# Weights of five more expert batches loaded before the expert stage, into the space of the residual and of the routing's row buffers

## The reference

```
E, K, I, CAP = 64, 8, 96, 64
probs = softmax(x @ gate_w.T);  w, sel = top_k(probs, K);  w = w / sum(w)
pos  = place of (token, expert) in its expert's queue;  valid = pos < CAP
xin[e, slot] = x[tok]                                   # 64 rows of each expert
h    = silu(xin @ wg) * (xin @ wu)                      # 256 -> 96
out  = h @ wd                                           # 96 -> 256
y[tok] += out[e, slot] * w * valid
return x + y
```

## Time and profile before

| | before |
|---|---|
| median of 3 runs | 1032.08 us (1030.96 to 1032.15) |
| profiled execution | 1035.25 us |
| its span in the trace | 1033.4 us |
| busy share of the span | PE 84%, DVE 65%, PEld 65%, ACT 41%, POOL 32% |
| DMA, SP's queue (plain) | 46.62 MB, 15.7% of 16 engines' span |
| DMA, POOL's queue (gathers and scatters) | 9.44 MB, 5.1% |

### The profile page before, as it was taken

The page is one execution under the profiler, slowest core; times in us unless marked ns, Lnnn a source line. Parts: engine busy times, 40 slices in busy tenths (PEclk is TensorE's granted clock), DMA queues, the critical chain, the costliest instruction groups (busy, mean ns, idle before and its releaser), DMA issues. The chain is left out here.

```text
span 1033.4 us, 25740 instructions
## 1 busy us (share of the span) xinstructions
PE 870.1 (84%) x9240; PEld 673.2 (65%) x9240; DVE 676.8 (65%) x1581; ACT 424.2 (41%) x1011; POOL 335.0 (32%) x293
## 2 busy tenths in 40 slices
PE   0799999999999899999889999999998840396881
PEld 0577777777777688998667777777776730264650
DVE  5577777777877665555367777777775589364560
ACT  1243444444434333324355566655556740021220
POOL 1443443434433040000133333333332010354763
PEclk9899999999999999999999999999999875598996
DMA  9300000000000000000011111111110396287542
GB/s 296 88 12 17 15 10 15 15 10 15 12 13 31 2 11 1 0 0 0 3 17 27 30 30 30 30 30 28 26 29 29 102 342 182 64 238 198 82 78 30
DMA packets 74906, 56.61 MB, mean 55 GB/s; under 512 B 40944, under 2 KB 70000, under 8 KB 74864
## 3 DMA queue, kind: packets, MB, share of 16 engines
q1 hardware_dynamic: 68720, 46.62, 15.7%
q0 software_dynamic: 6144, 9.44, 5.1%
HBM read 41.81 MB, written 14.22 MB: 54 GB/s over the span
## 5 line engine op out<-in xcount | busy, mean ns | idle before, releaser
L402 ACT ACTIVATE pr_t<-bank 128x512 f32<-128x512 f32 x128 | 76.4, 597 | 160.7 <-PE bank L298 159.9
L822 POOL TENSOR_TENSOR g_k_bd<-g_k_t,head_mask 128x1024 f32<-128x1024 f32 x32 | 60.6, 1895 | 134.8 <-ACT g_k_t L997 134.8
L310 PEld LDWEIGHTS bank<-v_bd,pr_t 128*64 128x64 f32 x2048 | 70.0, 137 | 26.5 <-issue 26.3
L298 PE MATMUL bank<-ident,sub 128*128 128x128 f32 x512 | 82.5, 284 | 3.6 <-ACT pr_t L402 2.9
L310 PE MATMUL bank<-v_bd,pr_t 128*64 128x18 f32 x2048 | 82.8, 214 | 0.1
L298 PEld LDWEIGHTS bank<-ident,sub 128*128 128x128 f32 x512 | 56.1, 141 | 31.3 <-issue 17.6
L479 DVE TENSOR_TENSOR sub<-bank,top 128x2048 f32<-128x2048 f32 x32 | 73.3, 2292 | 3.9 <-DVE top L475 0.2
L259 POOL TENSOR_TENSOR rot<-part_a,part_b 128x512 f32<-128x512 f32 x32 | 40.8, 1274 | 103.7 <-DVE part_b L488 103.7
L475 DVE TENSOR_REDUCE top<-bank 128x32 f32<-128x2048 f32 x32 | 73.1, 2285 | 0.6 <-PE bank L286 0.4
L817 POOL TENSOR_TENSOR xres<-xres,g_out_bias 128x256 f32 (+1 forms) x32 | 23.4, 731 | 152.4 <-DVE g_xn L1020 152.4
L646 ACT ACTIVATE f_hid<-bank,b 128x128 f32<-128x128 f32 x128 | 36.6, 368 | 85.4 <-PE bank L592 85.4
(11 more groups left out here) (196 smaller groups left out, 2040.0 us busy)
## 6 DMA issues: line engine op xcount, KB each, us to landing
e_w_gu<-in_experts_in SPq DMA_DIRECT2D x16, 768.0 KB, 9.0
e_w_d<-in_experts_out SPq DMA_DIRECT2D x16, 384.0 KB, 10.5
table<-r_row SPq DMA_DIRECT2D x16, 320.0 KB, 9.1
xres<-in_x SPq DMA_DIRECT2D x4, 1024.0 KB, 9.8
out<-xres SPq DMA_DIRECT2D x32, 128.0 KB, 1.7
keys_in<-in_ctx_t SPq DMA_DIRECT2D x32, 64.0 KB, 1.8
vals_in<-in_ctx_t SPq DMA_DIRECT2D x32, 64.0 KB, 1.8
w<-in_L_ffn_w SPq DMA_DIRECT2D x2, 1024.0 KB, 8.1
```

The source lines that it names most:

```text
L298: m = pe.transpose(b_pr[:, j * P:(j + 1) * P], sub[:, v, cols], k.ident[:, :])
L310: m = pe.matmul(b_o[64 * b:64 * b + 64, hp * VW0:(hp + 1) * VW0], pr_t[:, e, j, b * S:(b + 1) * S], v_bd[:, v, b, hp, :], start=True, stop ...
L402: act.activation(pr_t[:, e, :, :].rearrange("p j q -> p (j q)"), b_pr[:, :], ACT.Exp).then_inc(a_exp, 1)
L822: pool.tensor_tensor(k_bd[:, v, :, :, :, :].rearrange("p c b h s -> p (c b) h s"), k_t[:, v, :, :].rearrange("p c (b a s) -> p (c b) a s", ...
```

## The change

The places for weights become fourteen (`EARLY_E`): the nine of the ring, three in the space of `xres` (`OLD_E`), and two in new tiles `e_more_gu` and `e_more_d` (`MORE_E`), which are allocated after the tiles of the earlier stages are given back and so lie where the routing's `r_row` was. `load_experts` and the two matmuls take the place from `expert_weights`. SP issues the loads of batches 9 to 13 in the slot stage, behind waits for the last readers of the old contents; batches 14 and 15 go to the places of 0 and 1 in the expert stage.

```diff
 RING_E = 9
+OLD_E, MORE_E = 3, 2
+EARLY_E = RING_E + OLD_E + MORE_E
...
+def expert_weights(k, n):
+
+    wide, down = 4 * KC * 2 * I, 4 * D
+    place = n % EARLY_E
+    if place < RING_E:
+        return k.w_gu[:, place, :, :, :], k.w_d[:, place, :, :]
+    if place < RING_E + OLD_E:
+        at = (place - RING_E) * (wide + down)
+        old = k.xres[:, :, :].rearrange("p t d -> p (t d)")
+        return (old[:, at:at + wide].rearrange("p (e c i) -> p e c i", e=4, c=KC),
+                old[0:I, at + wide:at + wide + down].rearrange("i (e d) -> i e d", e=4))
+    return k.more_gu[:, place - RING_E - OLD_E, :, :, :], k.more_d[:, place - RING_E - OLD_E, :, :]
...
     def sync(sp):
         for n in range(NT // GT, RING_E):
             load_experts(sp, ins, k, n)
+        sp.wait_ge(k.r_xn, NT)
+        sp.wait_ge(k.out_set, 16 * NT)
+        for n in range(RING_E, RING_E + OLD_E):
+            load_experts(sp, ins, k, n)
+        sp.wait_ge(k.r_w, NT // GT)
+        sp.wait_ge(k.r_found, NT // GT)
+        sp.wait_ge(k.rows_set, 32 * (NT // GT))
+        for n in range(RING_E + OLD_E, EARLY_E):
+            load_experts(sp, ins, k, n)
...
         def sync(sp):
-            for n in range(RING_E, NB_E):
-                sp.wait_ge(e_gu, n - RING_E + 1)
-                sp.wait_ge(e_y, n - RING_E + 1)
+            for n in range(EARLY_E, NB_E):
+                sp.wait_ge(e_gu, n - EARLY_E + 1)
+                sp.wait_ge(e_y, n - EARLY_E + 1)
                 load_experts(sp, ins, k, n)
...
-                    pe.wait_ge(k.w_in[n % RING_E], 32 * (n // RING_E + 1))
+                    pe.wait_ge(k.w_in[n % EARLY_E], 32 * (n // EARLY_E + 1))
...
-        k.w_in = ring.sems(" ".join(f"e_w{n}" for n in range(RING_E)))
+        k.w_in = ring.sems(" ".join(f"e_w{n}" for n in range(EARLY_E)))
...
         k.w_gu, k.w_d = ring.sb("e_w_gu", [P, RING_E, 4, KC, 2 * I]), ring.sb("e_w_d", [I, RING_E, 4, D])
+        k.more_gu, k.more_d = z.sb("e_more_gu", [P, MORE_E, 4, KC, 2 * I]), z.sb("e_more_d", [I, MORE_E, 4, D])
```

More of the change, by code:

```diff
@@ L1100, in route @@
         b_turn, b_log, b_vals = [bank(0), bank(1)], [bank(5), bank(6)], [bank(2), bank(3)]
-        k.r_found = r_found
+        k.r_found, k.r_xn, k.r_w = r_found, r_xn, r_w
         groups = NT // GT
@@ L1240, in route @@
         return Stage(z.signals, sync=sync, gpsimd=gpsimd, tensor=tensor, scalar=scalar, vector=vector)
+def expert_weights(k, n):
[9 more added lines that the diff above has]
+    return k.more_gu[:, place - RING_E - OLD_E, :, :, :], k.more_d[:, place - RING_E - OLD_E, :, :]
 def load_experts(sp, ins, k, n):
     wide, down = 4 * KC * 2 * I, 4 * D
[L1247 to L1250, removed]
+    gate_up, back = expert_weights(k, n)
+    sp.dma_start(gate_up.rearrange("p e c i -> p (e c i)"), ins["experts_in"][:, n * wide:(n + 1) * wide]).then_inc(k.w_in[n % EARLY_E], 16)
+    sp.dma_start(back.rearrange("i e d -> i (e d)"), ins["experts_out"][:, n * down:(n + 1) * down]).then_inc(k.w_in[n % EARLY_E], 16)
 def fill_slots(nc, ins, k, bank, stack):
@@ L1409, in tensor @@
                         pe.wait_ge(e_part_s, n - 1)
+                    _, back = expert_weights(k, m)
                     for p in range(2):
@@ L1412, in tensor @@
                             mm = pe.matmul(b_y[halves[e], p * D:(p + 1) * D], hid_t[:, w, p, halves[e]],
-                                           k.w_d[:, m % RING_E, 2 * p + e, :], start=True, stop=True)
+                                           back[:, 2 * p + e, :], start=True, stop=True)
                     mm.then_inc(e_y, 1)
@@ L1416, in tensor @@
                     pe.wait_ge(e_gotTc, n + 1)
-                    pe.wait_ge(k.w_in[n % RING_E], 32 * (n // RING_E + 1))
+                    pe.wait_ge(k.w_in[n % EARLY_E], 32 * (n // EARLY_E + 1))
+                    gate_up, _ = expert_weights(k, n)
                     if n >= 2:
@@ L1423, in tensor @@
                                 mm = pe.matmul(b_gu[v][halves[e], p * 2 * I:(p + 1) * 2 * I], got_t[:, v, p, c, halves[e]],
-                                               k.w_gu[:, n % RING_E, 2 * p + e, c, :], start=(c == 0), stop=(c == KC - 1))
+                                               gate_up[:, 2 * p + e, c, :], start=(c == 0), stop=(c == KC - 1))
                     mm.then_inc(e_gu, 1)
```

## The result

| | before | with the change |
|---|---|---|
| median (10 runs each) | 1032.21 us (1030.96 to 1037.26) | 1024.21 us (1018.93 to 1029.37) |
| ratio of times | | 0.9913, 95% interval 0.9888 to 0.9937 |
| profiled execution | 1035.25 us | 1022.10 us |
| its span | 1033.4 us | 1020.3 us |

The change gains 9 us by the ratio (6.5 to 11.6), 8.0 by the medians; 1020.3 was forecast and 1018.0 to 1025.5 was the range. The ten times spread over 10.4 us, those of before over 6.3.

What follows compares the result with a forecast made beforehand. The expert stage was taken to wait on POOL's scatters, landing late beside weight loads. A gain of 11.8 us, all other terms 0, from the median 1032.08 gave 1020.3 us; range 1018.0 to 1025.5.

Steps and rivals of the forecast that it cites:

- Five loads leave the expert stage: Expert stage: without the loads of batches 9 to 13, scatters land sooner; gain 11.8 us, bounds 10.0 to 13.1.
- Periods 1 to 6: Expert stage, intervals between successive batches' first scatters on POOL, after the first interval: 6.50 us each, 39.00 instead of 50.76.
- Period 0: Expert stage, from the first batch's first scatter to the next batch's: stays 8.94 us, beside the two remaining loads.
- Five loads enter the slot stage at no cost: Slot stage: 5.90 MB at 327 to 290 GB/s end at 885.3 to 887.6, before the first gather; cost 0.
- the cover: Slot stage: spare time between the end of the moved loads and the first gather's issue at 889.70, 2 to 5 us.
- Rival 1: Start of expert stage: moved loads reach into the gathers, costing up to 5.2 us, time 1022 to 1025.5; chance 0.10.
- The new waits on SP at no cost: SP's queue in the slot stage: waits for residual and rows end early, some 16 us of cover; cost 0.
- DVE beside more transfers: Slot stage: DVE's search is equally fast with DMA engines full or idle, MAX8 2.29 us; cost 0.
- PE reads from other places: Expert matmuls: same shapes and order, five more semaphores cleared at the end; cost 0.
- Rivals 2, 3 and 4: In order: slow landings not from weights (1026.2 or 1032, 0.08); SP holding block's end (1040, 0.03); loads issued late (1028, 0.03).

Runs made afterwards that it cites:

- e2_no_late: Changed kernel without the expert-stage loads of batches 14 and 15, which reuse the weights of batches 0 and 1; 1020.96 us, ratio 0.9861.
- e4_before_no_late: Kernel before without its seven expert-stage loads; batches 9 to 15 reuse the weights of batches 0 to 6; 1020.25 us, ratio 0.9876.
- e8_before_paced: Kernel before, nine places, its seven late loads cut in three, two pieces released after each landing of scatters; 1023.24 us, ratio 0.988.
- e1_again: Changed kernel run again unaltered, for a second trace and more times; ratio 0.991 against the kernel before.
- e7_paced14: Changed kernel with the loads of batches 14 and 15 cut in three, one piece released after each landing of scatters; 1020.67 us, ratio 0.987.
- e11_contiguous: Changed kernel with each batch's weights laid out in one contiguous piece of HBM; 1023.01 us, ratio 0.9904.
- e5_front_more: Changed kernel with the weights of batch 0 loaded once more at the end of the slot stage; 1028.88 us, ratio 0.9949.
- e9_rows_last: Changed kernel with the sixteen row stores issued behind the first eight batches' loads instead of between them; 1022.37 us, ratio 0.9882.
- e3_old_only: Changed kernel with only the three places in the residual: batches 9 to 11 loaded early, 12 to 15 in the expert stage; 1023.31 us, ratio 0.9887.

## Why the prediction was right, and where a step was not

*Five loads leave the expert stage: right.* Periods 1 to 6 were forecast at 39.00 us and took 39.53 (916.11 to 955.64), before 50.76: a gain of 11.2 for 11.8. Period 0 kept 8.96 for 8.94, and e2_no_late shows that its excess is the two loads' (6.65 without them). The last eight periods took 52.46 where 52.00 was set. First to last scatter gained 10.75 us, 1.0 less than the sum has. That it is the weights and nothing else is shown by e4_before_no_late.

*Five loads enter the slot stage at no cost: this step failed in size.* I took 327 GB/s from a window in which row stores and loads alternate, and 290 as the slowest, from a window that was in part such a mix as well (its last rows, issued by 850.9, land up to 14.8 us later). Loads alone moved 245 GB/s in the profiled execution, and 221 to 276 in the full windows of the experiments up to e8_before_paced. The row that showed it stood in the earlier trace rows: 205 GB/s at a share of 0.78 is 263 for a full queue, and I used that window only to place the queue's end. At 245 GB/s the 5.90 MB take 24 us, not 18: the queue was dry at about 887, where the first gather is issued (887.09). Instead of 2 to 5 us the cover was about 2 us at best. With this order of loads the first gather landed after 4.57 (the profiled execution), 6.89 (e1_again), 9.11 (e2_no_late), 4.45 (e7_paced14) and 4.47 us (e11_contiguous): late in two traces of five, against 4.4 to 4.5 in the traces whose queue was dry long before.

*Rival 1 was therefore part of the truth.* Its price, up to 5.2 us for a first gather of up to 9.6 us, was about right (4.7 for 9.11), its chance of 0.10 too low. The median of 1024.2 lies in its interval of 1022 to 1025.5 and not in the forecast's own, which ended at 1022.5. So the stated range held only because rival 1's price was in it; the sum alone missed. The medians gained 8.0 us of 11.8: 1.0 of the 3.8 that are missing is in the periods, and late gathers took nearly nothing in one of the changed kernel's two traces and 2.3 us in the other. How much they take at the median is not shown.

The Trainium skill's rule (DMA: Bandwidth & Descriptors, Queues, rings and completion order) that a DMA engine serves its queues in turn, packet by packet, would make the gather take twice its time beside loads, 8.8 us. The traces with loads over most of the gather's way show 8.68 and 9.11 us, so they agree in size. Nor did the gather stand behind the loads: in e5_front_more the DMA engines still moved 233 GB/s from 890 to 892, and it landed at 893.41, much less than its own 4.4 us later.

*The new waits on SP at no cost: right.* SP was through at 861.6, some 22 us ahead of DVE's last instruction (883.77). The loads had no gap. *DVE beside more transfers: right*; from the first r_row instruction of POOL to that last one of DVE it took 68.5 us before and 68.3 after. *PE reads from other places: right*; from PE's first work to the first scatter it took 15.50 us before and 15.49 after.

*Rivals 2, 3 and 4* didn't come about.

## What to carry to other kernels

A transfer that is moved out of the way needs its cover reckoned at the rate of its own kind: take GB/s from a window in which only such transfers ran, and divide by the DMA share, since here a mix of stores and loads moved a quarter to a half more in one and the same trace (332 against 262 GB/s in e5_front_more, 353 against 228 in e2_no_late). Before giving a load more memory, try giving it a better time: cut into pieces that fit the idle part of a period and released by the event after which the DMA engines are idle, seven loads without a new place did no worse than fourteen places, and twelve places with four loads in pieces had a median 3.6 us below the first (on the same chip, with intervals that overlap) and 4.6 below the second. A wide spread of times after a change is a question and not an answer: here it led to the late gathers, but the granted clock went with it just as much, and e4_before_no_late spread over 8.5 us with no load near the gathers.

## What the hardware showed that I had not expected

**Loads alone are slower than loads and stores mixed, and not by a constant.** 327 to 403 GB/s for the mix at a share of 1.03 to 1.07, 221 to 276 for the loads of weights alone late in the slot stage, but 293 to 298 in e9_rows_last. The plain loads of the program's start (other tensors) moved 333 to 341 GB/s between 4 and 20 us in every trace. Spacing in HBM is excluded (e11_contiguous). What sets it stays open.

**TensorE's granted clock in the first expert batches differs from trace to trace.** PE starts the experts at 1.2 GHz (0.50), after some 50 us with almost no work. In the changed kernel's trace it has 2.4 GHz (1.00) at 897 and is back at 1.2 GHz at 900; in e3_old_only (second pair) it keeps 2.4 GHz:

```profile
897.00:898.00 1.00, 0.00 (x0) 0.00 (x0) 0.90 (x4) 0.00 (x0) 0.69 (x2) 1.00 0.49 123
900.00:902.00 2.00, 2.00 (x14) 1.30 (x12) 0.81 (x3) 0.00 (x0) 0.00 (x0) 0.50 0.28 82
```

```profile
897.00:898.00 1.00, 0.00 (x0) 0.00 (x0) 0.90 (x4) 0.00 (x0) 0.94 (x1) 1.00 0.50 143
900.00:902.00 2.00, 2.00 (x24) 1.43 (x20) 1.06 (x4) 0.00 (x0) 0.43 (x1) 1.00 0.51 142
```

From PE's first work to the first scatter it is then 13.2 us in e3_old_only and 15.0 to 16.8 in all others, 15.5 to 16.5 in the three that load the same twelve batches early. So some 2 to 3 us of a single trace can hang on this, and that reached one of my expectations. What decides it is not shown.
